# Two score banks per instruction, new engine orders, and no idle products in a gated cross-attention and mixture-of-experts block

## What is computed

```python
# LN: (x - mean) / sqrt(var + 1e-5)
# A: cross-attention to ctx, with a key mask
q, k, v = LN(x) @ Wq.T + bq, ctx @ Wk.T + bk, ctx @ Wv.T + bv        # 16 heads of 16
s = where(mask, -1e9, q @ k.T / 4);  o = softmax(s) @ v
x = x + tanh(g0) * (o @ Wo.T + bo)
# B: feed-forward block with rope, causal self-attention, 8 experts, top 2
y = LN(x);  q = k = rope(y);  v = y
o = softmax(where(causal, (q @ Wq.T) @ (k @ Wk.T).T / 4, -inf)) @ (v @ Wv.T)   # + biases
x1 = LN(y + o @ Wo.T + bo) * ln1_w + ln1_b
gates = softmax(x1 @ gate_w.T + gate_b);  best two kept
m = sum over the best two of gate_e * (x1 @ expert_w[e].T + expert_b[e])
x = x + tanh(g1) * (LN(x1 + m) * ln2_w + ln2_b)
```

## Time and profile before

| | |
|---|---|
| median of three runs | 829.53 us |
| the profiled execution | 829.5 us |
| its mean granted TensorE clock | 0.994 |
| instructions | 24325 |
| read from and written to memory | 14.99 and 4.19 MB, 23 GB/s |

### The profile page before, as it was taken

The page is one execution under the profiler, slowest core; times in us unless marked ns, Lnnn a source line. Parts: engine busy times, 40 slices in busy tenths (PEclk is TensorE's granted clock), DMA queues, the critical chain, the costliest instruction groups (busy, mean ns, idle before and its releaser), DMA issues.

```text
span 829.5 us, 24325 instructions
## 1 busy us (share of the span) xinstructions
PE 779.7 (94%) x9515; PEld 611.9 (74%) x9515; DVE 667.5 (80%) x1908; ACT 564.4 (68%) x1268; POOL 473.0 (57%) x854
## 2 busy tenths in 40 slices
PE   8888989999999999999999999999999999999896
PEld 4465768777787787778787788778778777777663
DVE  5756668797978979797988979797988979787876
ACT  5786767777786777777776777678677777764320
POOL 8434535566665646566574646566564655555343
PEclk9999999999999999999999999999999999999999
DMA  7510000010100101010100101010010000000000
GB/s 202 159 39 16 2 17 16 8 37 9 37 8 2 37 8 36 9 36 9 29 16 2 38 8 37 8 37 9 10 35 2 9 8 8 9 8 8 8 7 20
DMA packets 33570, 20.75 MB, mean 25 GB/s; under 512 B 11672, under 2 KB 33456, under 8 KB 33456
## 3 DMA queue, kind: packets, MB, share of 16 engines
q1 hardware_dynamic: 33456, 19.19, 8.1%
HBM read 14.99 MB, written 4.19 MB: 23 GB/s over the span
## 4 chain that ended last, share of the span: by engine, by line
PE 56%; ACT 24%; DVE 14%; issue 4%; POOL 1%; DMA 0%; SPq 0%; DVEq 0%; POOLq 0%
PE bank L395 26%; PE bank L516 8%; PE bank L535 7%; ACT bank L776 6%; DVE neg_max_A L1022 6%; ACT bank L785 5%; DVE moe L1131 4%; ACT probs_B L826 3%; PE bank L556 3%; PE bank L585 3%; ACT probs_A L826 3%; PE bank L574 2%; PE bank L404 2%; ACT k_heads_B L809 2%; PE bank L546 1%
## 5 line engine op out<-in xcount | busy, mean ns | idle before, releaser
L1343 POOL TENSOR_SCALAR_AFFINE_SELECT probs_B<-probs_B 128x512 f32<-128x512 f32 x128 | 77.3, 640 | 184.4 <-ACT probs_B L826 184.4
L1131 DVE SCALAR_TENSOR_TENSOR moe<-bank,gates,moe 128x256 f32<-128x256 f32 x256 | 123.2, 481 | 48.2 <-PE bank L395 33.2
L785 ACT ACTIVATE bank<-mask_add 128x512 f32<-128x512 bf16 x128 | 76.6, 602 | 49.2 <-DVE neg_max_A L1022 49.2
L395 PE MATMUL bank<-w_expertsa,u_t_a 128*128 128x512 f32 x256 | 105.6, 413 | 0.1
L395 PE MATMUL bank<-w_expertsa,u_t_b 128*128 128x512 f32 x256 | 100.9, 394 | 0.0
L395 PE MATMUL bank<-w_expertsb,u_t_a 128*128 128x512 f32 x256 | 100.9, 394 | 0.0
L1022 DVE TENSOR_REDUCE neg_max_A<-bank 128x4 f32<-128x512 f32 x128 | 79.5, 684 | 11.9 <-PE bank L516 11.5
L1022 DVE TENSOR_REDUCE neg_max_B<-bank 128x4 f32<-128x512 f32 x128 | 79.3, 682 | 5.5 <-PE bank L516 5.5
L776 ACT ACTIVATE bank<-mask_add 128x512 f32<-128x512 bf16 x128 | 69.8, 626 | 0.0
L776 ACT ACTIVATE bank<-causal_add 128x512 f32<-128x512 bf16 x128 | 69.7, 623 | 0.0
L826 ACT ACTIVATE probs_A<-bank 128x512 f32<-128x512 f32 x128 | 66.1, 603 | 4.4 <-PE bank L556 2.2
(11 more groups left out here) (224 smaller groups left out, 2440.5 us busy)
## 6 DMA issues: line engine op xcount, KB each, us to landing
x_in<-in_x SPq DMA_DIRECT2D x32, 128.0 KB, 2.2
ctx_t<-in_ctxT SPq DMA_DIRECT2D x32, 128.0 KB, 2.2
out<-y_out SPq DMA_DIRECT2D x32, 128.0 KB, 1.7
w_stage<-in_expertsT SPq DMA_DIRECT2D x8, 256.0 KB, 4.3
mask_u<-in_masks SPq DMA_DIRECT2D x32, 32.0 KB, 2.1
w_stage<-in_in_projT SPq DMA_DIRECT2D x3, 256.0 KB, 4.8
w_stage<-in_WkT SPq DMA_DIRECT2D x1, 256.0 KB, 3.5
w_stage<-in_WvT SPq DMA_DIRECT2D x1, 256.0 KB, 3.6
```

The costliest lines, as they stand in the source:

```text
L395: done = pe.matmul(out_ap, l, r, start=n == 0, stop=n == len(terms) - 1)
L785: act.activation(score_banks[g][:].rearrange("p (h k) -> p h k", k=P), mask_add[t % MASK_SLOTS][:, 1:2, :].to_broadcast([P, GROUP, P]), AC ...
L1131: dve.scalar_tensor_tensor(out=moe[(e + 1) % 2][:], in0=bank[:, (e % 2) * EMBED:(e % 2 + 1) * EMBED], scalar=gates[:, e:e + 1], in1=moe[e ...
L1343: pool.affine_select(out=part, in_=part, compare_op=ALU.is_ge, fill=0.0, base=0, pattern=[[0, GROUP], [1, P]], channel_multiplier=-1).then ...
```

## The change

- **Two banks an instruction.** The four score banks become one PSUM tensor `scores_ps`, and every ScalarE, VectorE and GpSimd step on scores or probabilities works on a piece of 8 heads, 1024 elements over two banks: 2 seeds, 2 reductions, 2 second seeds, 2 exponentials, 2 selects. TensorE's matmuls stay as they are; `scores` and `subtract_max` give one signal after the last matmul and no longer one a bank.
- **Maxima.** `max_parts` writes 4 heads for each strip (16 elements in place of 64), and `pick` shrinks from 16 to 4 rows of heads. `pick` and its `strip_rows` are now made by VectorE, with memsets of `neg_max_bf`.
- **Orders.** All five engine lists and `WORK_USES` are new. `o_raw` exists once for A and once for B. `attend` for B, `project_v_b`, `transpose_max`, `o_transposed` and the bias product now claim their bank with `take_work`; `project_k_a` does not. A `B_v` projection waits for its split. `finish` on GpSimd is cut in two (`keep`, `finish`). GpSimd's lags are larger numbers, and the rounds are 16 + 12; the added rounds do nothing on the other engines.
- **Loads.** SyncE's loads are spread over rounds 0 to 4: tile 0, Ak, tile 1, Av, then Aq and so on.
- **No idle products.** `keep_busy` and its 167 matmuls are gone.
- Further semaphores (`c_causal`, `c_tanh`, `w_small`, `c_fold_2`, `kept`, `A_res` for `base_a`) order setup and small steps that had no wait of their own.

```diff
-SCORES = (("A", 1, 1), ("B", 1, 2), ("A", 0, 0), ("B", 0, 1))
+SCORES = (("A", 0, 3), ("B", 0, 4), ("A", 1, 3), ("B", 1, 4))
...
+        def score_piece(c):
+
+            return scores_ps[:, c * PIECE_BANKS:(c + 1) * PIECE_BANKS, :].rearrange("p g (h k) -> p (g h) k", k=P)
...
+            def seed_scores_t(c, t):
+                if not live(t):
+                    return
+                act.wait_ge(sem["A_max"], PIECES * t + c + 1)
+                act.activation(score_piece(c), mask_add[t % MASK_SLOTS][:, 1:2, :].to_broadcast([P, PIECE_HEADS, P]),
+                               ACT.Copy).then_inc(sem["A_seed_t"], 1)
...
+            def exponentials(tag, c, t):
+                if not live(t):
+                    return
+                act.wait_ge(sem[tag + "_sm"], t + 1)
+                act.activation(probs[tag][:, c * PIECE_HEADS:(c + 1) * PIECE_HEADS, :], score_piece(c), ACT.Exp,
+                               scale=SCALE).then_inc(sem[tag + "_exp"], 1)
...
+            def maxima(tag, c, t):
+                if not live(t):
+                    return
+                dve.wait_ge(sem[tag + "_s"], t + 1)
+                dve.tensor_reduce(neg_max[tag][:, c * PIECE_HEADS:(c + 1) * PIECE_HEADS], score_piece(c), AXIS_X, ALU.max,
+                                  negate=True).then_inc(sem[tag + "_max"], 1)
```

More of the change, by code:

```diff
@@ L23 @@
 STRIP = 32
+PIECES = 2
+PIECE_BANKS = GROUPS // PIECES
+PIECE_HEADS = HEADS // PIECES
 EXPERTS = 8
@@ L230, in build @@
         y_out = sb("y_out", [P, EMBED])
-        banks = [ctx.enter_context(nc.psum_tensor(f"bank{i}", [P, BANK], F32)) for i in range(8)]
-        score_banks, work_banks = banks[0:GROUPS], banks[GROUPS:8]
+        scores_ps = ctx.enter_context(nc.psum_tensor("scores_ps", [P, GROUPS, BANK], F32))
+        work_banks = [ctx.enter_context(nc.psum_tensor(f"bank{i}", [P, BANK], F32)) for i in range(GROUPS)]
         def live(t):
@@ L453, in project_v_a, with project_pair @@
                          [tuple(w[:, c, :] for w in weight["Av"]) for c in range(CHUNKS)]).then_inc(sem["A_v_mm"], 1)
-            def project_pair(mat, parts, pair):
-                bank = take_work(f"{mat[0]}_{mat[1]}", pair)
+            def project_pair(bank, mat, parts):
                 for m in range(CHUNKS):
@@ L534, in scores_t @@
                             i = 2 * c + odd
-                            pe.matmul(score_banks[g][:, i * P:(i + 1) * P], keys[strip, half, c, odd, :],
-                                      queries[strip, half, c, :], start=tag == "B" and i == 0, stop=False,
-                                      skip_group_check=True)
+                            done = pe.matmul(scores_ps[:, g, i * P:(i + 1) * P], keys[strip, half, c, odd, :],
+                                             queries[strip, half, c, :], start=tag == "B" and i == 0, stop=False,
+                                             skip_group_check=True)
+                done.then_inc(sem[tag + "_st"], 1)
             def transpose_max(tag, t):
@@ L584, in normalise @@
                 for g in range(GROUPS):
-                    done = pe.transpose(bank[:, g * P:(g + 1) * P], o_raw[:, g * P:(g + 1) * P], ident[:])
+                    done = pe.transpose(bank[:, g * P:(g + 1) * P], o_raw[tag][:, g * P:(g + 1) * P], ident[:])
                 done.then_inc(sem[tag + "_or_tp"], 1)
@@ L831, in raw_values @@
                     return
-                other, tile = before(RAW, tag, t)
                 act.wait_ge(sem[tag + "_pv"], t + 1)
-                act.activation(o_raw[:], work_bank(tag + "_values", t)[:], ACT.Copy).then_inc(sem[tag + "_or"], 1)
+                act.activation(o_raw[tag][:], work_bank(tag + "_values", t)[:], ACT.Copy).then_inc(sem[tag + "_or"], 1)
             def gates_transposed(t):
@@ new lines, in scalar_program @@
+                keep_queries("B", r - 4)
+                if r == 4:
+                    small_parts()
+                high_u(2 * r - 10)
+                high_o("B", 2 * r - 9)
+                raw_values("A", 2 * r - 6)
+                if r == 4:
+                    split_high("E1")
+                    split_high("E2")
+                max_transposed("B", 2 * r - 8)
+                high_o("A", 2 * r - 6)
+                gate_exponentials(2 * r - 10)
+                exponentials("B", 0, 2 * r - 8)
@@ L1299, in rope, with keep @@
                 pool.tensor_tensor(roped[:], roped[:], rope_tmp[:], ALU.add).then_inc(sem["rope3"], 1)
+            def keep(t):
+                if not live(t):
+                    return
+                if t == 0:
+                    pool.wait_ge(sem["c_fold_2"], 2)
+                kept = x1[t % X1_SLOTS]
+                pool.tensor_tensor(kept[:], kept[:], rows["ln2_b"][:], ALU.add).then_inc(sem["kept"], 1)
             def finish(t):
```

982 lines of the change are left out of this document (490 added, 492 removed).

## The result

The changed kernel takes 864.34 us (median of 4 runs, 864.03 to 864.89) against 829.71 (828.97 to 829.95) for the kernel before on the same chip: a ratio of 1.0419, with an interval of 1.0405 to 1.0434. It is slower by 4.2%, where I forecast 807 us and gave 785 to 832 as the range. The profiled execution has a span of 863.0 us.

The account below looks back on a forecast made before the run. The prediction took TensorE as the bound, 42.1 us of a 47.17 us round, with 5.1 us of stalls. From 829.5 us, -27 for 14 rounds and +5 for head and tail gave 807 us, range 785 to 832.

Parts of the forecast that it names:

- TensorE's waits on the score buffer go, and the new order wins 1.9 us a round.: TensorE's order: hand-over stalls fall from 3.4 to 1.5 us a round; the merges themselves win nearly nothing.
- the 45.2 of the sum: Steady rounds: the forecast period in us, down from 47.17, giving -27 us over 14 rounds.
- A wide instruction costs the slope alone.: Two-bank score steps: the second half adds only its elements, 0.43 us on ScalarE, not a full second instruction of 0.60.
- the larger 187 ns: ScalarE's merged seeds: estimated saving per pair from paying SBUF source latency once, 1.1 us more a round over 12 pairs.
- The maxima's parts: another 0.6 off VectorE.: Parts of the maxima on VectorE: shrinking from 64 to 16 elements saves another 0.6 us a round.
- Coarser hand-over: 0.5 us more per entry of A.: Scores of A to their transposed scores: one signal after all 16 matmuls lengthens the path from 4.33 to 4.85 us.
- The causal select on GpSimd becomes two wider pieces and stays hidden: GpSimd's select on B: no cost, as 4.5 us or more of TensorE work stand between subtraction and attend.
- VectorE's order eats the gain: Rival, chance 0.22: VectorE's list comes late to the reductions; period 46.2 to 47.2 us, time 821 to 834 us.
- More bank claims: cost 0.: TensorE's work banks: added claims wait on readers already some us old; cost 0, at most a small piece like 0.3.
- No idle products: +12 for the clock, -6 for their time.: Head and tail: lower TensorE clock adds 12 us; removing the products from the tail's chain saves 6 us.
- cold TensorE: Rival, chance 0.12: without products the clock stays low through most of head and tail; costs 31 us, time 834 us.
- Loads: -1.: Head: weights issued tile by tile, Ak ahead of the second tile, shorten the first split's wait by 1 us.

Follow-up runs that it names:

- e3: The changed kernel with GpSimd's select of B replaced by a one-element copy, so probabilities above the diagonal stay uncleared; 825.0 us, ratio 0.9936 to the kernel before.
- e4: The changed kernel with GpSimd's select in four pieces of 512 elements, as in the kernel before; 852.1 us, ratio 1.0258 to the kernel before.
- e6: The kernel before with ScalarE and VectorE score steps over two banks, its orders, TensorE signals and select kept; 839.4 us, ratio 1.0107.
- e7: The changed kernel with 163 idle products put back in rounds 0 to 2 and 16 to 18; 847.9 us, ratio 1.0211 to the kernel before.
- e11: The changed kernel with GpSimd's key_bias and make_lower moved behind the first two tiles' context parts; 860.6 us, ratio 1.0366 to the kernel before.

## Why the prediction was wrong

Three kernels split the 33.5 us of span into steps: before, before without its products (e1, span 850.0), after without the select (e3, span 820.4), after (863.0).

| step | forecast | span | medians |
|---|---|---|---|
| no idle products | +6 | +20.5 | +19.5 |
| order, two banks, bank claims, loads | -28 | -29.6 | -24.4 |
| the select's effect on VectorE | 0 | +42.6 | +39.3 |

The profiled executions of e1 (the slowest of its four) and e3 (the fastest of its five) lie at opposite ends, so the medians are the better measure; they sum to 34.3. This is one path through the edits, not a proof that each costs so much in any order; but the products agree from both ends (19.5 and 16.5 us), and the hold fits e4, where 36% of the holding goes and 31% of the time comes back. That the second line comes near its forecast is partly luck. I had put 27 of the 28 us in the rounds. From e1 to e3 the 13 rounds gain 19.9, the tail gains 14.2, of which I had foreseen nothing, and the head loses 4.5.

- *TensorE's waits on the score buffer go, and the new order wins 1.9 us a round.* Right in kind, close in size: without the select the period is 45.5 us in the last six rounds against the 45.2 of the sum, 1.6 under the 47.16 of e1, and 45.70 over all 13. The score bank left TensorE's list of waits.
- *A wide instruction costs the slope alone.* Right. The reduction takes 1217 to 1219 ns (forecast 1210), the exponential 1035 (forecast 1040); ScalarE is busy 531 us in place of 564. The select, whose probabilities lie in SBUF and in no bank, takes 1097 in place of 640. Two seeds of 1024 take 1.98 us in place of 2.18 for four: 0.10 a merged pair, as the rows gave it; the larger 187 ns that the prediction estimated did not show.
- *The maxima's parts: another 0.6 off VectorE.* Wrong. The four instructions of an A and a B tile take 0.79 us in before and 0.96 in after, since the copy to bf16 is held beside GpSimd's products (mean 381 ns for A, 184 before). That is 0.3 us a round more.
- *Coarser hand-over: 0.5 us more per entry of A.* Right: 0.49, by e6. I let it vanish in the sum because the new order covers it. In the old order the wide instructions as a whole cost 9.3 us.
- *"The causal select on GpSimd becomes two wider pieces and stays hidden".* This is the step that failed. The words are true of TensorE: none of its waits from 200 to 600 us in after names the select. I asked whom the select's result makes wait, and not what the select does to its neighbours while it runs. I had priced VectorE as 40.5 less 1.1 us, a sum of durations from the old order, and those durations weren't properties of the instructions alone: VectorE takes 42.3 us a round with the select and 39.0 without (e3). The trace of before had the warning: `gates`, a step of a fixed shape, takes 0.23 us in one tile and 0.53 in the next.
- *The rival "VectorE's order eats the gain"* had the right engine and the wrong mechanism. It allowed 1.0 to 2.0 us a round for late reductions and ended at 834. Held instructions cost 3.3 us of VectorE a round, and the period rose by 2.4 over e3's (48.07 against 45.70); with the tail that is 42.6 us of span (39.3 by the medians), far outside the case.
- *More bank claims: cost 0.* After's waits of `w_Ava` and the other projections for `x` and `u_n` look like a refutation (8.3 and 4.8 us). But in e3, with the same claims, they are gone. So the claims show no cost while VectorE is on time, and passed its lateness on when it wasn't.
- *No idle products: +12 for the clock, -6 for their time.* The mechanism was right and the size wrong. Measured, net, +16.5 (e7) and +19.5 (e1) in place of +6. I took the share of low clock of the last stretch, 22%, as the share in the whole head, though before is at 0.89 there with products around it. In after the head has 0.59 and 0.88 where before has 1.00. And the 5.9 us that were to come off in the tail did not show: e1's tail is 10.6 longer. The rival "cold TensorE" priced this at +31 by itself; the truth lies between it and the forecast.
- *Loads: -1.* The start went the other way, by 3.7 us (e11), and not through the loads' order, which no run prices by itself. I looked at what the weights' load releases and didn't walk down GpSimd's new list, where the first wait is for the load of the biases, and the first split stands behind it.

So even with the clock and the start right (+19.5 and +3.7 in place of +6 and -1), the forecast would have been at about 826, still faster; without the select the changed kernel takes 825.0 (e3). The sign turned on the hold.

## What to carry to other kernels

Before reordering VectorE or GpSimd, lay the two lists beside each other in time: where a VectorE instruction with two tensors in SBUF (or one like `gates`, `v_n` or the copy of the maxima) falls beside a long GpSimd one, its price is the rest of that instruction. In a trace, compare the shortest and the longest of one shape on one engine; if they differ twofold, as `gates` did in before (the comparisons of after differ fivefold), durations from the old order don't carry over to the new. Move the steps that nobody awaits, those that read PSUM, or reductions and statistics beside the long ones, and then look for whom that makes late.

Idle products that keep TensorE's clock are to be priced by removing them, not by the time that they fill.

## What was not expected of the hardware

- A 64-element comparison on VectorE takes 0.22 us alone, 0.65 beside selects of 512 elements and 1.10 beside selects of 1024: the hold follows the other engine's instruction, not its own size. The 8- and 24-element steps are held as well (`chosen` 0.85, 0.15 alone; `gates` 1.02, 0.23 alone). A reduction, a reciprocal or statistics with one tensor in SBUF are not (`rank` 0.22, `gate_inv` 0.15, `stats_B` 0.43, as without a select).
- Without idle products the granted clock from 20 to 60 us fell to 0.59 (after) and 0.67 (e1), with TensorE shown as busy for 28.05 and 24.19 of 40 us; with them it is 1.00 (e7) at 35.56. Some 165 products of 512 columns buy 16.5 to 19.5 us.
- Instructions over two banks cost only their elements on ScalarE and VectorE: the second 512 elements add 432 ns to an exponential and 533 to a reduction, 0.84 and 1.04 ns an element, the slopes within one bank (0.86 and 1.04). No run shows a charge for the border.
